# Another written-out order of the cycle of a cross-attention kernel, from sequence 2 on

## The chip, the cores and the metric

The kernel runs on one core of a Trainium2 chip. The metric is the device time of one execution in microseconds (us), the median of several runs.

## What is computed

The layer normalises the input of each of 16 sequences, forms queries from it and keys and values from a context, and adds the attention of 8 heads to the input (cut to what matters; n = 16, c = 64 channels, s = 256 positions, h = 8):

```python
def reference(input, context, gamma, beta, Wq, bq, Wkv, bkv, Wo, bo):
    mu, var = mean(input, axis=(1, 2)), var(input, axis=(1, 2))
    xn = (input - mu) * rsqrt(var + EPS) * gamma[:, None] + beta[:, None]
    q = einsum('oc,ncs->nos', Wq, xn) + bq[:, None]
    kv = einsum('od,nds->nos', Wkv, context) + bkv[:, None]
    ...
    att = softmax(einsum('nhqc,nhkc->nhqk', q * c**-0.25, k * c**-0.25))
    y = einsum('nhqk,nhkc->nhqc', att, v)
    return input + einsum('co,nos->ncs', Wo, y.reshaped) + bo[:, None]
```

## The kernel before, in words

Precision is kept by splitting operands into a high and a low part. For each sequence the work falls into small steps, each a function of the program with the sequence and a head, a unit or a half as arguments. The products of Wq and Wk (t, in `t_a` high and `t_b` low) replace queries and keys, and the products of Wv and Wo (u, in `u_hi` and `u_lo`) replace values and output projection.

TensorE (PE) has `turn_of_t(m, k)` (four matmuls into the bank `ps_t`: t of four heads), `maxima(m, unit)` (one matmul of 512 columns into one of two banks `ps_max`: first scores, from the high parts, only for the row maximum), `transpose_max(m, 0)` (turns the maxima of all heads), `scores(m, head)` (four matmuls into one of two banks `ps_sc`), `values_of_context(m, kt)` (two matmuls into `ps_m`: u), `values(m, first)` (24 short matmuls: the exponentials of two heads by u, into one of two banks `ps_z`) and `transposed_sum(m)` (turns the summed heads into `ps_t`).

ScalarE (ACT) has `t_high` (t_a out of ps_t), `exponentials(m, head)` (two activations over the same scores: `p_hi` in fp16, then `p_full` in fp32), `u_high`, `transpose_out` (the turned maxima, which it then also sends by a DMA of its own queue into a row of `t_b`, so that `scores` subtracts the maximum) and small `inputs`. VectorE (DVE) has `t_low`, `reduce_max(m, unit)`, `u_low`, `reciprocals(m, first)` (of the sums of exponentials of two heads), `add_values(m, first)` (four small instructions that scale and add these two heads) and `residual(m)`. GpSimd (POOL) forms `p_lo` = p_full - p_hi of every head, except for six of the last eleven that DVE does (`p_low`). SyncE (SP) issues all other copies, up to three that replicate t_a within the core (L400, L414), one for t_b (L406), c_pad and c_seq (the context), x_seq and the output. SP waits in program order too, and its order isn't touched.

Sequences overlap. Every engine works through its own written-out list, and semaphores make it wait. For the first two sequences the order comes from tables (`step`); from there on each engine runs `cycle(n)` for n = 1 to 14, then `last(15)`. In a cycle stand steps of the sequences n - 2 to n + 2. `fresh` skips a step that has already been issued. So a cycle is the unit of the steady state, and there are twelve of them between the residual of sequence 0 and that of sequence 12. The waits that matter below:

```python
need(pe, dve_tlo, t_bank_free(turn))      # turn_of_t: t_low of the turn before is done (one bank ps_t)
need(pe, act_p, m * H + head - 1)         # scores: the exponentials two heads before are done
pe.wait_ge(dma_negmax[q], 16 * neg_max_loads(m))   # scores(m, 0): the row of maxima has landed
need(pe, dve_max, m * H + unit - 1)       # maxima: reduce_max two units before is done
pe.wait_ge(dve_max, (m + 1) * H)          # transpose_max: all eight reduce_max of m are done
act.wait_ge(dma_tb[q][k], 16 * fills(m))  # transpose_out, before its DMA: both copies of t_b have landed
dve.wait_ge(dve_inv, m * PAIRS + pair + 1)  # add_values: its own reciprocals are done
```

Of the kernel before, what the change touches and what calls it, by code (L numbers as in the profile page):

```python
# [78 lines left out]
def xattn_program(nc, x2_in, x_tiles_in, ctx2_in, wq_in, wk_in, w_in, out):  # L79
# [4 lines left out]
    with stack:  # L84
# [247 lines left out]
        def fresh(done, kind, index, within=True):  # L332

            if not within or index < done.get(kind, 0) or kind == 't' and index >= PAIRS + 2 * (N - 1):
                return False
            done[kind] = index + 1
            return True
# [89 lines left out]
        def _(pe):  # L427
# [136 lines left out]
            def maxima(m, unit):  # L564

                if not fresh(done, 'max', m * H + unit, 0 <= m < N):
                    return
                q, bank = m % 2, unit % 2
                need(pe, dve_max, m * H + unit - 1)
                if m == 0:  # L570
                    if unit == 0:
                        c_ready(pe, m)
                    if unit < 2:
                        pe.wait_ge(dve_alo, unit + 1)
                    if unit % 2 == 0:
                        pe.wait_ge(act_thi, unit // 2 + 1)
                    for qt in range(KT):
                        last = mm(ps_max[:, bank, qt * S:(qt + 1) * S], t_a[:, q, unit, qt * P:(qt + 1) * P], c_seq[:, m % C_BUFS, 0, :],
                                  start=True, stop=True)
                else:  # L580
                    if unit == 0:
                        pe.wait_ge(dma_cpad[q], 32 * fills(m))
                    if unit % 4 == 0:
                        pe.wait_ge(act_thi, PAIRS + 2 * (m - 1) + unit // 4 + 1)
                    head, qt = unit // 2 * 2, unit % 2
                    last = mm(ps_max[:, bank, :], t_a[:, q, head, qt * P:(qt + 1) * P], c_pad[:, q, :, :].rearrange("p k s -> p (k s)"),  # L586
                              start=True, stop=True)
                last.then_inc(pe_s1, 1)

            def transposed_sum(m):  # L590

                if not fresh(done, 'y', m, 0 <= m < N):
                    return
                pe.wait_ge(dve_zsum, (m + 1) * H * KT)
                need(pe, dve_tlo, min(PAIRS + 2 * (m + 3 - 1) + 2, PAIRS + 2 * (N - 1)))
                nc.tensor.transpose(ps_t[:, 0:P], z_sum[:, m % 2, :, :].rearrange("p t c -> p (t c)"), ident[:]).then_inc(pe_y, 1)  # L596
# [51 lines left out]

            def cycle(n):

                maxima(n + 1, 2)
                maxima(n + 1, 3)
                scores(n, 0)
                values(n - 1, 4)
                scores(n, 1)
                maxima(n + 1, 4)
                maxima(n + 1, 5)
                scores(n, 2)
                values(n - 1, 6)
                transposed_sum(n - 2)  # L660
                scores(n, 3)
                maxima(n + 1, 6)
                maxima(n + 1, 7)
                values_of_context(n + 1, 0)
                turn_of_t(n + 2, 0)
                scores(n, 4)
                values(n, 0)
                maxima(n + 2, 0)
                transpose_max(n + 1, 0)
                maxima(n + 2, 1)  # L670
                scores(n, 5)
                scores(n, 6)
                values_of_context(n + 1, 1)
                values(n, 2)
                scores(n, 7)
                turn_of_t(n + 2, 1)

            def last(n):

                scores(n, 0)  # L680
                values(n - 1, 4)
                scores(n, 1)
                scores(n, 2)
                values(n - 1, 6)
                transposed_sum(n - 2)
                scores(n, 3)
                values_of_context(n, 1)
                scores(n, 4)
                values(n, 0)
                scores(n, 5)  # L690
                scores(n, 6)
                values(n, 2)
                scores(n, 7)
                transposed_sum(n - 1)
                values(n, 4)
                values(n, 6)
                transposed_sum(n)
# [5 lines left out]
        def _(act):  # L703
# [65 lines left out]
            def t_high(m, k):  # L769

                turn = turn_of(m, k)
                if not fresh(done, 't', turn):
                    return
                act.wait_ge(pe_t, turn + 1)
                need(act, pe_s2, (m - 2) * H + 4 * k + 4)
                to = t_a[:, 0, 2 * k:2 * k + 2, :] if m == 0 else packed(t_a, m, k)[:, 0]
                nc.scalar.activation(to, t_bank(turn).rearrange("p (j s) -> p j s", j=2), ACT.Copy).then_inc(act_thi, 1)  # L777
# [48 lines left out]

            def cycle(n):

                t_high(n + 1, 1)
                u_high(n, 1)  # L830
                exponentials(n, 0)
                inputs(n, 0)
                exponentials(n, 1)
                inputs(n, 1)
                exponentials(n, 2)
                inputs(n, 2)
                exponentials(n, 3)
                u_high(n + 1, 0)
                t_high(n + 2, 0)
                inputs(n, 3)  # L840
                exponentials(n, 4)
                transpose_out(n + 1, 0)
                inputs(n, 4)
                exponentials(n, 5)
                inputs(n, 5)
                exponentials(n, 6)
                inputs(n, 6)
                exponentials(n, 7)
                inputs(n, 7)

            run_cycles(step, cycle, cycle)


# [66 lines left out]
        def _(dve):  # L920
# [184 lines left out]

            def cycle(n):

                reduce_max(n + 1, 1)
                add_values(n - 1, 2)
                reduce_max(n + 1, 2)  # L1110
                p_low(n - 1, 7)
                reduce_max(n + 1, 3)
                u_low(n, 1)
                reciprocals(n - 1, 4)
                t_low(n + 1, 1)
                reduce_max(n + 1, 4)
                p_low(n, 1)
                reduce_max(n + 1, 5)
                residual(n - 2)
                add_values(n - 1, 4)  # L1120
                reduce_max(n + 1, 6)
                p_low(n, 3)
                reduce_max(n + 1, 7)
                u_low(n + 1, 0)
                reciprocals(n - 1, 6)
                reciprocals(n, 0)
                add_values(n - 1, 6)
                t_low(n + 2, 0)
                reduce_max(n + 2, 0)
                p_low(n, 5)  # L1130
                add_values(n, 0)
                reciprocals(n, 2)

            def last(n):
# [61 lines left out]
```

## Time and profile before

| | us |
|---|---|
| median of 3 runs | 220.38 (219.92, 220.38, 222.49) |
| the profiled execution | 218.92 |
| its span, first to last instruction | 217.1 |
| twelve cycles, residual to residual | 136.04, so 11.34 each |
| after the twelfth | 22.2 |

The profiled execution is 1.46 below the median of the runs. Its busy shares are PE 93%, DVE 92%, ACT 83%, POOL 75% of the span. A busy PE in this profile is partly a model of the ends of matmuls, so that waits of PE are better read from starts of instructions. The granted TensorE clock is full (1.0) in all of the cycles.

### The profile page before, as it was taken

What the parts mean: (1) busy time and instruction counts of PE and PEld (TensorE: products, weight loads), DVE (VectorE), ACT (ScalarE), POOL (GpSimd) and SP (SyncE); (2) the same over time, 40 slices, a digit from 0 to 9 for tenths busy, and PEclk for the clock granted to TensorE, in tenths of its full rate; (3) what the DMA queues carried; (4) which work ended last, traced back from release to release, by engine and by line L of the source; (5) the groups of instructions that cost most, each with busy time, mean ns of one, the idle gap of its engine ahead of it and who ended that gap; (6) DMA issues with size and microseconds to landing.
All of it is one profiled execution on the core that took longest, in us unless ns stands there. A gap on an engine that the chain in (4) does not pass through costs nothing.

```text
span 217.1 us, 7194 instructions
## 1 busy us (share of the span) xinstructions
PE 202.1 (93%) x2511; PEld 178.1 (82%) x2511; DVE 199.2 (92%) x589; ACT 180.1 (83%) x366; POOL 162.6 (75%) x162
## 2 busy tenths in 40 slices
PE   6987888899999999999999999999999999999882
PEld 6876766788888888898989987988988898988771
DVE  4589998899999999999999999999999999997884
ACT  2365588797989898989899898989898989898980
POOL 5136087896989888888889889889787879786550
PEclk9975899999999999999999999999999999999997
DMA  5963137672765757667566665666666574552000
GB/s 147 295 259 89 37 73 170 140 160 64 161 160 132 168 128 169 139 156 163 133 158 150 160 152 127 147 151 161 145 148 160 127 176 113 128 116 47 2 22 17
DMA packets 31090, 29.04 MB, mean 134 GB/s; under 512 B 4240, under 2 KB 29840, under 8 KB 31056
## 3 DMA queue, kind: packets, MB, share of 16 engines
q1 hardware_dynamic: 30224, 28.07, 54.5%
q10 hardware_dynamic: 832, 0.53, 0.9%
q8 instruction: 20, 0.33, 0.7%
q14 instruction: 14, 0.11, 0.2%
HBM read 3.80 MB, written 1.05 MB: 22 GB/s over the span
## 4 chain that ended last, share of the span: by engine, by line
PE 78%; DVE 8%; ACT 6%; DMA 3%; issue 2%; ACTq 1%; SPq 0%
PE ps_sc L559 16%; PE ps_sc L560 13%; PE ps_max L586 12%; PE ps_z L508 7%; PE ps_z L510 7%; PE ps_z L509 7%; PE ps_m L622 3%; PE ps_m L623 3%; DMA x_res<-x_tiles 3%; PE ps_t L532 3%; PE ps_t L533 3%; ACT p_full L790 2%; DVE neg_max L1020 1%; ACT p_hi L787 1%; PE ps_t L596 1%
## 5 line engine op out<-in xcount | busy, mean ns | idle before, releaser
L913 POOL TENSOR_TENSOR p_lo<-p_full,p_hi 128x512 f16<-128x512 f32 x122 | 139.6, 1166 | 30.4 <-ACT p_full L790 26.3
L787 ACT ACTIVATE p_hi<-ps_sc 128x512 f16<-128x512 f32 x128 | 78.7, 615 | 14.7 <-PE ps_sc L560 13.2
L1020 DVE TENSOR_REDUCE neg_max<-ps_max 128x2 f32<-128x512 f32 x128 | 82.8, 677 | 1.5 <-PE ps_max L586 1.3
L790 ACT ACTIVATE p_full<-ps_sc 128x512 f32<-128x512 f32 x128 | 79.2, 618 | 0.5 <-POOL p_lo L913 0.5
L559 PE MATMUL ps_sc<-t_a,c_seq 128*128 128x256 f32 x256 | 72.4, 306 | 2.4 <-issue 1.6
L560 PE MATMUL ps_sc<-t_b,c_seq 65*128 65x256 f32 x256 | 66.4, 282 | 0.0
L559 PEld LDWEIGHTS ps_sc<-t_a,c_seq 128*128 128x128 f32 x256 | 49.1, 192 | 9.7 <-ACT p_full L790 4.2
L508 PE MATMUL ps_z<-u_hi,p_hi 128*128 128x65 f16 x512 | 53.4, 195 | 1.2 <-DVE p_lo L1066 1.1
L508 PEld LDWEIGHTS ps_z<-u_hi,p_hi 128*128 128x128 f16 x512 | 45.9, 97 | 8.6 <-issue 5.1
L509 PE MATMUL ps_z<-u_lo,p_hi 128*128 128x64 f16 x512 | 52.8, 192 | 0.0
L510 PE MATMUL ps_z<-u_hi,p_lo 128*128 128x65 f16 x512 | 52.7, 193 | 0.0
L560 PEld LDWEIGHTS ps_sc<-t_b,c_seq 65*128 65x128 f32 x256 | 48.8, 190 | 0.9
L1040 DVE SCALAR_TENSOR_TENSOR z_sum<-ps_z,inv_sum,z_sum 128x64 f32<-128x64 f32 x224 | 48.2, 274 | 0.1
L509 PEld LDWEIGHTS ps_z<-u_lo,p_hi 128*128 128x128 f16 x512 | 46.7, 98 | 0.0
L510 PEld LDWEIGHTS ps_z<-u_hi,p_lo 128*128 128x128 f16 x512 | 46.7, 97 | 0.0
L586 PE MATMUL ps_max<-c_pad,t_a 128*128 128x512 f32 x120 | 41.4, 417 | 0.6 <-DVE neg_max L1020 0.2
L1058 DVE TENSOR_TENSOR u_lo<-ps_m,u_hi 128x512 f16<-128x512 f32 x32 | 21.9, 685 | 1.2 <-ACT u_hi L799 1.1
L586 PEld LDWEIGHTS ps_max<-c_pad,t_a 128*128 128x128 f32 x120 | 19.8, 190 | 2.9 <-DVE neg_max L1020 1.5
L1000 DVE TENSOR_TENSOR t_b<-ps_t,t_a 128x512 fp32r<-128x512 f32 (+1 forms) x30 | 20.1, 671 | 0.0
L799 ACT ACTIVATE u_hi<-ps_m 128x512 f16<-128x512 f32 x32 | 19.5, 610 | 0.6 <-PE ps_m L623 0.6
L777 ACT ACTIVATE t_a<-ps_t 128x512 fp32r<-128x512 f32 x30 | 18.3, 608 | 0.0
L532 PE MATMUL ps_t<-x_seq,a_hi 128*128 128x256 f32 x60 | 16.1, 290 | 0.3 <-issue 0.3
(107 smaller groups left out, 231.3 us busy)
## 6 DMA issues: line engine op xcount, KB each, us to landing
t_a<-t_a SPq DMA_DIRECT2D x90, 128.0 KB, 2.5
t_b<-t_b SPq DMA_DIRECT2D x30, 128.0 KB, 2.5
x_seq<-x_hi SPq DMA_DIRECT2D x15, 128.0 KB, 2.4
c_pad<-c_hi SPq DMA_DIRECT2D x30, 64.0 KB, 2.0
c_seq<-c_hi SPq DMA_DIRECT2D x15, 128.0 KB, 2.4
x_res<-x_tiles SPq DMA_DIRECT2D x4, 256.0 KB, 6.2
out<-x_res SPq DMA_DIRECT2D x16, 64.0 KB, 2.1
x_seq<-x_lo SPq DMA_DIRECT2D x15, 64.0 KB, 2.1
```

The costliest lines, as they stand in the source:

```text
L508: mm(ps_z[:, bank, z0:z0 + Z_W], p_hi[:, buf, kt, qs], u_h, start=(kt == 0), stop=False)
L509: mm(ps_z[:, bank, z0:z0 + C], p_hi[:, buf, kt, qs], u_l, start=False, stop=False)
L510: last = mm(ps_z[:, bank, z0:z0 + Z_W], p_lo[:, buf, kt, qs], u_h, start=False, stop=(kt == KT - 1))
L532: mm(bank[:, j * S:(j + 1) * S], a_hi_cols[:, first:first + 2 * C], x_seq[:, q, 0, :], start=True, stop=False)
L559: mm(ps_sc[:, bank, kt * S:(kt + 1) * S], c_seq[:, b, 0, keys], t_a[:, q, head, :], start=True, stop=False)
L560: last = mm(ps_sc[:, bank, kt * S:(kt + 1) * S], c_seq[0:C + 1, b, 1, keys], t_b[0:C + 1, q, head, :], start=False, stop=True)
L586: last = mm(ps_max[:, bank, :], t_a[:, q, head, qt * P:(qt + 1) * P], c_pad[:, q, :, :].rearrange("p k s -> p (k s)"), start=True, stop=True)
L787: nc.scalar.activation(p_hi[:, buf, :, :].rearrange("p t s -> p (t s)"), scores, ACT.Exp).then_inc(act_phi, 1)
L790: nc.scalar.activation(p_full[:, head % 2, :], scores, ACT.Exp).then_inc(act_p, 1)
L913: nc.gpsimd.tensor_tensor(p_lo[:, buf, :, :].rearrange("p t s -> p (t s)"), p_full[:, head % 2, :], p_hi[:, buf, :, :].rearrange("p t s -> ...
L1020: nc.vector.tensor_reduce(to, ps_max[:, unit % 2, :].rearrange("p (t s) -> p t s", t=KT), X, ALU.max, negate=True).then_inc(dve_max, 1)
L1040: nc.vector.scalar_tensor_tensor(out=total, in0=part, scalar=scale, in1=total, op0=ALU.mult, op1=ALU.add).then_inc(dve_zsum, 1)
```

## The change

The three lists `cycle(n)` are written in another order. Nothing is added or removed: the same steps run on the same engines. The list `last(n)` of PE loses `scores(n, 0)`, since the cycle before has it now.

```diff
 PE: def cycle(n):
-                maxima(n + 1, 2)
                 maxima(n + 1, 3)
-                scores(n, 0)
                 values(n - 1, 4)
+                maxima(n + 1, 4)
                 scores(n, 1)
-                maxima(n + 1, 4)
                 maxima(n + 1, 5)
+                transposed_sum(n - 2)
                 scores(n, 2)
+                maxima(n + 1, 6)
                 values(n - 1, 6)
-                transposed_sum(n - 2)
+                values_of_context(n + 1, 0)
                 scores(n, 3)
-                maxima(n + 1, 6)
+                turn_of_t(n + 2, 0)
                 maxima(n + 1, 7)
-                values_of_context(n + 1, 0)
-                turn_of_t(n + 2, 0)
                 scores(n, 4)
                 values(n, 0)
+                transpose_max(n + 1, 0)
                 maxima(n + 2, 0)
-                transpose_max(n + 1, 0)
                 maxima(n + 2, 1)
                 scores(n, 5)
+                values(n, 2)
                 scores(n, 6)
                 values_of_context(n + 1, 1)
-                values(n, 2)
+                maxima(n + 2, 2)
                 scores(n, 7)
                 turn_of_t(n + 2, 1)
+                scores(n + 1, 0)
 ACT: def cycle(n):
-                t_high(n + 1, 1)
-                u_high(n, 1)
-                exponentials(n, 0)
-                inputs(n, 0)
                 exponentials(n, 1)
                 exponentials(n, 2)
+                u_high(n + 1, 0)
                 exponentials(n, 3)
-                u_high(n + 1, 0)
                 t_high(n + 2, 0)
...
                 exponentials(n, 7)
+                t_high(n + 2, 1)
                 inputs(n, 7)
+                exponentials(n + 1, 0)
+                u_high(n + 1, 1)
+                inputs(n + 1, 0)
 DVE: def cycle(n):
-                reduce_max(n + 1, 1)
                 add_values(n - 1, 2)
                 reduce_max(n + 1, 2)
                 reduce_max(n + 1, 3)
-                u_low(n, 1)
+                t_low(n + 1, 1)
                 reciprocals(n - 1, 4)
-                t_low(n + 1, 1)
                 reduce_max(n + 1, 4)
+                residual(n - 2)
+                u_low(n, 1)
                 reduce_max(n + 1, 5)
-                residual(n - 2)
-                add_values(n - 1, 4)
                 reduce_max(n + 1, 6)
+                add_values(n - 1, 4)
+                reciprocals(n - 1, 6)
+                u_low(n + 1, 0)
                 reduce_max(n + 1, 7)
-                u_low(n + 1, 0)
-                reciprocals(n - 1, 6)
+                add_values(n - 1, 6)
                 reciprocals(n, 0)
-                add_values(n - 1, 6)
-                t_low(n + 2, 0)
+                add_values(n, 0)
                 reduce_max(n + 2, 0)
-                add_values(n, 0)
+                reduce_max(n + 2, 1)
+                t_low(n + 2, 0)
                 reciprocals(n, 2)
```

In three places the instructions themselves show it. The line numbers of the changed kernel are one lower from here on for ACT and DVE.

PE at the end of a cycle, before: the turn of t (L532, L533), two maxima (L586), then the scores of head 0 (L559, L560).

```order
L532 MATMUL ps_t<-x_seq,a_hi 128x256
L533 MATMUL ps_t<-x_seq,a_lo 128x256
L532 MATMUL ps_t<-x_seq,a_hi 128x256
L533 MATMUL ps_t<-x_seq,a_lo 128x256
L586 MATMUL ps_max<-c_pad,t_a 128x512 x2
L559 MATMUL ps_sc<-t_a,c_seq 128x256
L560 MATMUL ps_sc<-t_b,c_seq 128x256
```

PE at the same place in the changed kernel:

```order
L532 MATMUL ps_t<-x_seq,a_hi 128x256
L533 MATMUL ps_t<-x_seq,a_lo 128x256
L532 MATMUL ps_t<-x_seq,a_hi 128x256
L533 MATMUL ps_t<-x_seq,a_lo 128x256
L559 MATMUL ps_sc<-t_a,c_seq 128x256
L560 MATMUL ps_sc<-t_b,c_seq 128x256
L559 MATMUL ps_sc<-t_a,c_seq 128x256
L560 MATMUL ps_sc<-t_b,c_seq 128x256
L586 MATMUL ps_max<-c_pad,t_a 128x512
```

Scores of head 0 follow the turn of t at once, one of the maxima comes after them, and the other one has moved ahead of the turn.

ACT where a sequence ends and the next begins, before: the exponentials of head 7, `t_high` (L777), `u_high` (L799), the exponentials of head 0.

```order
L787 ACTIVATE p_hi<-ps_sc 128x512
L790 ACTIVATE p_full<-ps_sc 128x512
L777 ACTIVATE t_a<-ps_t 128x2x256
L799 ACTIVATE u_hi<-ps_m 128x8x64
L787 ACTIVATE p_hi<-ps_sc 128x512
L790 ACTIVATE p_full<-ps_sc 128x512
```

ACT there in the changed kernel:

```order
L786 ACTIVATE p_hi<-ps_sc 128x512
L789 ACTIVATE p_full<-ps_sc 128x512
L776 ACTIVATE t_a<-ps_t 128x2x256
L786 ACTIVATE p_hi<-ps_sc 128x512
L789 ACTIVATE p_full<-ps_sc 128x512
L798 ACTIVATE u_hi<-ps_m 128x8x64
```

`u_high` has moved behind the exponentials of head 0.

DVE in the second half of a cycle, before: from `u_low(n + 1, 0)` (L1058) by the two reciprocals (L1011), `add_values(n - 1, 6)` (L1040), `t_low(n + 2, 0)` (L1000), a reduction (L1020), `add_values(n, 0)` (L1037, L1040), and on to `add_values(n, 2)`.

```order
L1058 TENSOR_TENSOR u_lo<-ps_m,u_hi 128x512
L1011 RECIPROCAL inv_sum<-ps_z 128x4 x2
L1040 SCALAR_TENSOR_TENSOR z_sum<-ps_z,inv_sum,z_sum 128x64 x4
L1000 TENSOR_TENSOR t_b<-ps_t,t_a 128x2x256
L1020 TENSOR_REDUCE neg_max<-ps_max 128x2
L1037 TENSOR_SCALAR z_sum<-ps_z,inv_sum 128x64 x2
L1040 SCALAR_TENSOR_TENSOR z_sum<-ps_z,inv_sum,z_sum 128x64 x2
L1011 RECIPROCAL inv_sum<-ps_z 128x4
L1020 TENSOR_REDUCE neg_max<-ps_max 128x2
L1040 SCALAR_TENSOR_TENSOR z_sum<-ps_z,inv_sum,z_sum 128x64 x4
```

DVE there in the changed kernel:

```order
L1057 TENSOR_TENSOR u_lo<-ps_m,u_hi 128x512
L1019 TENSOR_REDUCE neg_max<-ps_max 128x2
L1039 SCALAR_TENSOR_TENSOR z_sum<-ps_z,inv_sum,z_sum 128x64 x4
L1010 RECIPROCAL inv_sum<-ps_z 128x4
L1036 TENSOR_SCALAR z_sum<-ps_z,inv_sum 128x64 x2
L1039 SCALAR_TENSOR_TENSOR z_sum<-ps_z,inv_sum,z_sum 128x64 x2
L1019 TENSOR_REDUCE neg_max<-ps_max 128x2 x2
L999 TENSOR_TENSOR t_b<-ps_t,t_a 128x2x256
L1010 RECIPROCAL inv_sum<-ps_z 128x4
L1039 SCALAR_TENSOR_TENSOR z_sum<-ps_z,inv_sum,z_sum 128x64 x4
```

Two of the four reciprocals of a cycle now stand directly ahead of the sum that uses them, and `t_low(n + 2, 0)` has moved from before `add_values(n, 0)` to behind it and behind two reductions.

## Rows read from the trace of the kernel before

**Rows 1.** Windows from residual to residual: window, length; busy us of the engines
```profile
58.83:70.23 11.40, 11.37 (x152) 10.11 (x151) 11.13 (x33) 10.48 (x22) 10.29 (x11) 1.00 0.64 150
...
104.39:115.63 11.24, 11.24 (x152) 10.04 (x151) 11.02 (x34) 10.36 (x23) 9.77 (x10) 1.00 0.62 142
...
183.56:194.87 11.31, 11.25 (x152) 10.04 (x151) 11.01 (x33) 10.40 (x22) 9.25 (x9) 1.00 0.56 125
```

**Rows 2.** Timeline of a cycle, ACT and PE: start, us, instruction, idle before
```profile
101.10 0.62 ACT L799 ACTIVATE u_hi<-ps_m 128x512 f16<-128x512 f32 x1
102.05 0.64 ACT L790 ACTIVATE p_full<-ps_sc 128x512 f32<-128x512 f32 x1
102.74 0.19 PEld L559 LDWEIGHTS ps_sc<-t_a,c_seq 128*128 128x128 f32 x1 [0.39 <-ACT p_full L790]
110.11 0.36 PE L559 MATMUL ps_sc<-t_a,c_seq 128*128 128x256 f32 x1
```

**Rows 3.** Timeline of DVE in the same cycle
```profile
101.14 0.68 DVE L1020 TENSOR_REDUCE neg_max<-ps_max 128x2 f32<-128x512 f32 x1
101.75 0.69 DVE L1058 TENSOR_TENSOR u_lo<-ps_m,u_hi 128x512 f16<-128x512 f32 x1
102.35 0.17 DVE L1011 RECIPROCAL inv_sum<-ps_z 128x4 f32<-128x4 f32 x1
102.44 0.66 DVE L1000 TENSOR_TENSOR t_b<-ps_t,t_a 128x512 fp32r<-128x512 f32 x1
...
104.39 0.35 DVE L1049 SCALAR_TENSOR_TENSOR x_res<-ps_t,u_unscale,x_res 128x128 f32<-128x128 f32 x1
104.66 0.85 DVE L1040 SCALAR_TENSOR_TENSOR z_sum<-ps_z,inv_sum,z_sum 128x64 f32<-128x64 f32 x4
105.43 1.28 DVE L1020 TENSOR_REDUCE neg_max<-ps_max 128x2 f32<-128x512 f32 x2
```

**Rows 4.** Timeline of DVE at the end of the kernel
```profile
213.08 0.18 DVE L1011 RECIPROCAL inv_sum<-ps_z 128x4 f32<-128x4 f32 x1
213.30 0.86 DVE L1040 SCALAR_TENSOR_TENSOR z_sum<-ps_z,inv_sum,z_sum 128x64 f32<-128x64 f32 x4
```

**Rows 5.** Timeline of PE, one step of each kind (of values, the first matmul)
```profile
99.93 0.62 PE L586 MATMUL ps_max<-c_pad,t_a 128*128 128x512 f32 x2
100.39 0.28 PE L559 MATMUL ps_sc<-t_a,c_seq 128*128 128x256 f32 x1
...
100.87 0.20 PE L508 MATMUL ps_z<-u_hi,p_hi 128*128 128x65 f16 x1
...
101.60 0.37 PE L559 MATMUL ps_sc<-t_a,c_seq 128*128 128x256 f32 x1
```

**Rows 6.** The copy of the maxima, its scores, and its 15 landings (view of L764)
```profile
130.68 0.54 ACTq L764 DMA_DIRECT2D t_b<-neg_max_rows  x1
...
133.61 0.63 PE L586 MATMUL ps_max<-c_pad,t_a 128*128 128x512 f32 x2
134.69 0.36 PE L559 MATMUL ps_sc<-t_a,c_seq 128*128 128x256 f32 x1 [0.45 <-issue]
...
DMA to landing us min/median/max: 1.8/2.5/3.9
```

**Rows 7.** SP's copies of t_b in two cycles, and their 30 landings (view of L406)
```profile
98.21 0.61 SPq L406 DMA_DIRECT2D t_b<-t_b  x1
...
103.54 0.60 SPq L406 DMA_DIRECT2D t_b<-t_b  x1
...
131.52 0.62 SPq L406 DMA_DIRECT2D t_b<-t_b  x1
...
138.27 0.61 SPq L406 DMA_DIRECT2D t_b<-t_b  x1
...
DMA to landing us min/median/max: 2.4/2.5/4.1
```

**Rows 8.** Timeline of ACT in the last sequence, exponentials of head 3
```profile
205.85 0.60 ACT L787 ACTIVATE p_hi<-ps_sc 128x512 f16<-128x512 f32 x1 [0.23 <-PE ps_sc L560]
```

More of the change, by code:

```diff
@@ L649, in cycle @@
             def cycle(n):
-                maxima(n + 1, 2)
                 maxima(n + 1, 3)
-                scores(n, 0)
                 values(n - 1, 4)
+                maxima(n + 1, 4)
                 scores(n, 1)
-                maxima(n + 1, 4)
                 maxima(n + 1, 5)
+                transposed_sum(n - 2)
                 scores(n, 2)
+                maxima(n + 1, 6)
                 values(n - 1, 6)
-                transposed_sum(n - 2)
+                values_of_context(n + 1, 0)
                 scores(n, 3)
-                maxima(n + 1, 6)
+                turn_of_t(n + 2, 0)
                 maxima(n + 1, 7)
-                values_of_context(n + 1, 0)
-                turn_of_t(n + 2, 0)
                 scores(n, 4)
                 values(n, 0)
+                transpose_max(n + 1, 0)
                 maxima(n + 2, 0)
-                transpose_max(n + 1, 0)
                 maxima(n + 2, 1)
                 scores(n, 5)
+                values(n, 2)
                 scores(n, 6)
                 values_of_context(n + 1, 1)
-                values(n, 2)
+                maxima(n + 2, 2)
                 scores(n, 7)
                 turn_of_t(n + 2, 1)
+                scores(n + 1, 0)
             def last(n):
-                scores(n, 0)
                 values(n - 1, 4)
```

## The prediction

> **What bounds the kernel now.** I read the busy time from residual to residual first. An undisturbed cycle takes 11.24 us, the first of the twelve 11.40, and their mean is 136.04 / 12 = 11.34; in 11.24 us DVE is busy 11.02 and ACT 10.36 [rows 1]. So the reader should see three engines close to full, and ask for the loop that closes a cycle, not for the busiest engine. The timeline shows it: PE stands 0.39 us until `exponentials(n, 0)` is done, starts `scores(n, 2)` about 102.75, and runs from there without a wait to `scores(n, 7)` at 110.11, which is 7.36 us [rows 2]. The other 3.9 us of the loop are ACT's: exponentials of head 7, `t_high`, `u_high`, exponentials of head 0. DVE isn't the bound, only close to it. Its own sum goes by starts: a reduction 0.61, `u_low` 0.60, a reciprocal 0.09, the residual 0.27, the four instructions of `add_values` 0.77 [rows 3]; `t_low` is taken as 0.60 like `u_low`. Eight reductions 4.8 (two in a row take 1.2, so 0.60 each), two `t_low` and two `u_low` 2.4, four `add_values` 3.08, four reciprocals 0.36, residual 0.27: 10.9. DVE waits about 0.34 us a cycle.
>
> **ACT: the old loop opens.** With `u_high(n, 1)` behind the exponentials of head 0, those start 0.47 us earlier (one such start to the next, 0.95 for `u_high` and the first of the two exponentials together) [rows 2]. If nothing else held, a cycle would be 10.8. `u_low(n, 1)` comes later on DVE as well, so nobody waits for `u_high` there.
>
> **DVE: 0.26 us more of its own.** A reciprocal takes 0.09 when something else follows; where its own sum follows it takes 213.30 - 213.08 = 0.22 [rows 3, 4]. Two of four now stand so: +0.26, sum 11.14 a cycle. The waits it has today may go, for `values(n, 0)` and `transposed_sum` now stand further ahead of what needs them. The Trainium skill (VectorE: DVE Perf Modes, "The DRAIN you can't avoid") says that a semaphore after each DVE operation costs nothing extra; by it DVE's sum would stay at 10.9. The rows disagree, and I take the rows.
>
> **A new loop, DVE to PE to DVE.** `turn_of_t(n + 2, 1)` needs the bank that `t_low(n + 2, 0)` reads, and this now comes late on DVE, after `add_values(n, 0)` and two reductions. Behind that turn PE has `scores(n + 1, 0)` and `maxima(n + 2, 3)`, and DVE's `reduce_max(n + 2, 3)` waits for the latter. Call the start of `reduce_max(n + 1, 3)` zero. Until the end of `t_low(n + 2, 0)` DVE does seven reductions 4.2, `t_low` and two `u_low` 1.8, three `add_values` 2.31, three reciprocals 0.40 (one at 0.22), the residual 0.27, and the last `t_low` 0.66: 9.64. Then the turn, four matmuls like scores, 0.48 (from 100.39 to 100.87) [rows 5], up to 0.58 if its first weights are loaded after a wait; scores 0.48; the maximum 0.43 until it can be read (two take 0.62 with starts 0.23 apart, and a little for the signal). With 0.05 to 0.12 for the signal to PE this is 11.08 to 11.25.
>
> **PE nearly fills it too.** By starts [rows 5]: maxima 0.23, scores 0.48, values 0.73, a turn 0.48, the context 0.46, and 0.08 where long weights follow short matmuls. Eight, eight, four, two and two of these, with five of the 0.08 and 0.15 for the two transpositions: 11.0. Laid out from zero, `maxima(n + 1, 3)` starts at -0.43, `scores(n, 3)` at 3.7, `scores(n, 4)` at 4.9, `values(n, 0)` at 5.4; `transpose_max` at 6.1 has to wait for `reduce_max(n + 1, 7)`, which ends at 6.08 and signals by 6.2; the turn is reached at 9.8, when `t_low` has just ended (9.64 and the signal). PE meets DVE within 0.1 us twice a cycle. The closed loop by this path is 11.15 to 11.25. I take 11.22 for the new cycle, in the upper half, since each such meeting can only add. Against 11.24 that is -0.02 x 12 = -0.2 us. The ends are 11.14 (DVE alone: -0.1 x 12 = -1.2) and 11.35 (another 0.1 for the two meetings: +1.3). So the loop of ACT is replaced by another of the same length.
>
> **Queues that are passed: the copy of the maxima.** `scores(n, 0)` waits for the row of maxima that ACT sends. One such copy was issued at 130.68; two maxima started at 133.61, and scores would have followed 0.46 later, at 134.07. They started at 134.69 [rows 6]. The row calls it "issue", but 130.68 + 3.9, the longest landing, is 134.58: it is the landing. The slack is 134.07 - 130.68 = 3.39; three landings of the cycles are longer (3.8, 3.9 and about 3.5), and cost 0.4 + 0.5 + 0.1 = 1.0 us. In the new order: exponentials of head 3 start about 0.7 after their scores (0.48 for four matmuls and the drain of the last), at 4.4; they take 0.96, `t_high` 0.48, those of head 4 0.96, `transpose_out` 0.3. The copy goes out at 7.1, and `scores(n + 1, 0)` is due at 9.64 + 0.12 + 0.53 = 10.3. The slack is 3.2, 0.2 less.
>
> And ACT may not issue it before SP's second copy of t_b has landed. Today SP issues this at 103.54 - 101.14 = 2.4 after zero [rows 3, 7], far ahead. Its chain of copies starts with the other copy of t_b, which must wait for `t_low(n + 2, 0)`, in the new order at 9.64 - 11.22 = -1.6. From the one copy to the other SP takes 5.33 in one cycle and 6.75 in another [rows 7]. So the second goes out at 3.8 to 5.2 and lands (2.5 in the median) at 6.3 to 7.7, against 7.1: up to 0.6 of wait on ACT, 0.2 in the mean. Behind it are queued the exponentials of heads 5 to 7, which have some 0.3 us of slack against PE. With 0.2 less slack and 0.2 more delay, the spread of the landings (three of thirteen at 3.5 to 3.9, one 3.1, nine up to 2.6) gives 0.20 us a cycle in place of 0.08: +1.5. If no landing is long, it is -1.0. What speaks for shorter ones is that SP now stands idle for over a microsecond before `t_low(n + 2, 0)`, so less is under way beside the row. I take the middle, +0.25.
>
> The Trainium skill (DMA: Bandwidth & Descriptors, "Anatomy of one DMA — SWDGE (gpsimd) path") calls the fixed 2 us of a transfer roughly constant, and this row is 8 KB. By it the landing would never matter, and the term would be -1.0. The view has 1.8 to 3.9 for equal copies [rows 6], so the spread, not the fixed part, is what decides here.
>
> **The end.** From `cycle(14)` on no new maxima and turns are left, and ACT is the chain. There `u_high(15, 1)` stood before the exponentials of head 0 as well; PE got `scores(15, 2)` later and ACT still waited 0.23 before head 3 [rows 8]. Moving it gives between 0 and 0.48; I take -0.4, since that wait shows that PE's side was late for it.
>
> **Sum**, against the profiled execution: 218.92 - 0.2 + 0.25 - 0.4 = 218.6. The runs' median is 1.46 above the profiled execution, so 220.0. POOL, the other copies and the first two sequences are set at nothing: the heads' p_lo are due 0.5 us or more after POOL has them, but the margin for `values(n, 2)` shrinks from some 2 us to 0.6, and there its cover ends; one more GpSimd instruction of 0.7 there would cost 0.1.
>
> **Rivals.** (A) DVE alone sets the cycle and no row is late. For it: both meetings are within what the rows resolve, and SP's idle time. -1.2 - 1.0 - 0.4 = -2.6: 216.3, so 217.8 as a median. If the page's rule on semaphores held too, the new loop would lose a further 0.13 a cycle, and 216.2 would be possible. Against it: any 0.1 us of jitter now hits an engine without slack.
>
> (B) Slower: the copy of the maxima becomes the bound. Its place is the wait of `scores(n + 1, 0)`, its cause SP's later copy of t_b, its price 12 times the mean lateness, behind which maxima 3 and DVE's reduction stand. It decides from 0.03 us a cycle above what I took, and is visible (2%) from 0.4. With a lateness of 0.5 in every cycle (landings at 3.4, issue 0.3 late): 12 x 0.5 = 6.0 in place of today's 1.0, so 218.92 - 0.2 + 5.0 - 0.4 = 223.3, as a median 224.8; with half of it 221.8.
>
> (C) The two meetings cost 0.1 us each: +2.4 above the forecast, 222.4. It differs from B by where PE stands: before the turn and before `transpose_max`.
>
> **Chances.** Forecast (a cycle of 11.15 to 11.30, rows late as now) 0.5, A 0.2, B 0.18, C 0.12. The range takes all of A's but its far end, C, and the milder half of B: 217.2 to 223.2. Two per cent is 4.4 us, about what a measurement of this kernel tells from no change. Below 216.0 lies only the far end of A, 0.03; above 224.8 the upper part of B, 0.07; in between 0.9.
>
> **What the changed profile would show.** Residuals 11.22 apart, with no wait of PE before `scores(n, 2)`. DVE busy above 11.1 a cycle: its reciprocals 0.22 apart from their sums twice a cycle. PE reaching `turn_of_t(n + 2, 1)` as `t_low` ends. Copies of the maxima issued 7.1 us after `reduce_max(n + 1, 3)`, scores of head 0 3.2 later; where PE stands longer there, the landing, and ACT idle before this copy, speak for B. I am wrong if DVE's chain or PE's has a wait I put at zero, and most easily if the landings shift as a whole.

## The result, and the profile after

The changed kernel took 222.72 us (median of 4 runs, 221.96 to 224.15), the kernel before 220.15 beside it: a ratio of 1.0111, 95% interval [1.0066, 1.0156]. Two further copies of it, each timed beside before, gave 1.001 [0.997, 1.005] and 1.0091 [1.0047, 1.0134]. The same code thus gives 0.1 to 1.1% in three comparisons, which differ by more than their intervals. It is slower by some tenths of a per cent to one per cent, where 220.0 had been forecast with the sign of a small gain. The profiled execution took 222.15 us, its span 220.3.

I split the spans of this profile, of two others of the same code and of a second one of the kernel before by the residuals, as in [rows 1]:

| profile | span | first residual | twelve cycles | of these the first | a clean cycle | cycles 2 to 12 above clean |
|---|---|---|---|---|---|---|
| before | 217.1 | 58.83 | 136.04 | 11.40 | 11.24 | 1.0 |
| before, repeated (c_before) | 218.4 | 60.23 | 135.89 | 11.47 | 11.24 | 0.8 |
| after | 220.3 | 60.99 | 135.91 | 10.73 | 11.15 | 2.5 |
| after, repeated (c_after) | 219.8 | 57.26 | 139.21 | 10.57 | 11.15 | 6.0 |
| after, repeated (c_after2) | 218.7 | 59.23 | 136.04 | 10.58 | 11.15 | 2.8 |

The last column is the sum of cycles 2 to 12 less eleven clean ones. In the changed cycle the residual stands 1.4 us earlier (1.87 behind `reduce_max(n + 1, 3)`, before 3.25 [rows 3]), that of sequence 0 only 0.8 (3.69 against 4.50). So the starts are better compared by `reduce_max(3, 3)` itself: it begins at 54.3 and 55.8 us in the two profiles of the kernel before, at 57.3, 53.6 and 55.6 in the three of the changed one. Over all fourteen profiles of this document the mean is 55.9 for the old order and 55.9 for the new one: the start varies by itself. From there to the end it is 162.8 and 162.6 us before, and 163.1, 166.2 and 163.1 after. So of the 3.2 us between the first profiles of the two kernels 3.0 lie at the start. What the change did is in the last two columns: **clean cycles got shorter, and the time lost in disturbed ones grew.**

Windows of the changed kernel, columns as in [rows 1]: a clean cycle, and a disturbed one.

```profile
94.54:105.70 11.16, 11.16 (x152) 10.29 (x151) 11.09 (x34) 10.18 (x22) 9.67 (x10) 1.00 0.66 152
...
162.15:173.66 11.51, 11.48 (x152) 10.23 (x151) 11.12 (x35) 10.12 (x22) 9.22 (x9) 1.00 0.64 144
```

DVE is busy 11.09 of 11.16 us, where it was 11.02 of 11.24 [rows 1]: it has its longer sum, and hardly any wait. In the disturbed cycle it is busy for the same time (11.12), and the cycle is 0.35 longer. Why is seen on the timelines of SP, ACT, PE and DVE there:

```profile
163.43 1.90 SPq L414 DMA_DIRECT2D t_a<-t_a  x1
165.38 0.61 SPq L406 DMA_DIRECT2D t_b<-t_b  x1
...
167.03 0.25 ACT L753 ACTIVATE neg_max_rows<-ps_m 16x128 fp32r<-16x128 f32 x1
167.94 0.52 ACTq L763 DMA_DIRECT2D t_b<-neg_max_rows  x1
168.56 0.60 ACT L786 ACTIVATE p_hi<-ps_sc 128x512 f16<-128x512 f32 x1 [1.28 <-PE ps_z L510]
169.06 0.59 ACT L789 ACTIVATE p_full<-ps_sc 128x512 f32<-128x512 f32 x1
...
169.27 0.40 PE L586 MATMUL ps_max<-c_pad,t_a 128*128 128x512 f32 x1
169.70 0.39 PE L559 MATMUL ps_sc<-t_a,c_seq 128*128 128x256 f32 x1
...
171.33 0.40 PE L586 MATMUL ps_max<-c_pad,t_a 128*128 128x512 f32 x1
...
171.77 0.69 DVE L1019 TENSOR_REDUCE neg_max<-ps_max 128x2 f32<-128x512 f32 x1 [0.32 <-PE ps_max L586]
```

SP's second copy of t_b goes out at 165.38, 5.1 behind `reduce_max(n + 1, 3)` (160.28, the residual's 162.15 less 1.87), and needs 2.47: it lands at 167.85. ACT has turned the maxima at 167.03 and could send them 0.28 later, at 167.31, as in the undisturbed cycles. It sends them at 167.94, so 0.63 late and 0.10 behind that landing; in all seven cycles of this profile where ACT sends the row late, it does so 0.10 behind the landing of this copy. So it waited for that. The row of ACT names PE as the releaser of its idle time, but the DMA that stands between is what was waited for. Behind it ACT is 0.63 late: exponentials of head 5 end at 169.65, so `scores(n, 7)` starts at 169.70, where it would follow its maximum after 0.23, at 169.50; then the turn, `scores(n + 1, 0)`, maxima 3, and DVE waits 0.32 for these. Of 0.63 us of ACT's wait, 0.32 reach the cycle.

The other wait is that for the row itself. Where it lands in time, `scores(n + 1, 0)` starts 3.19 us behind the copy's issue (3.40 in the kernel before); here in after and in before:

```profile
99.70 0.52 ACTq L763 DMA_DIRECT2D t_b<-neg_max_rows  x1
...
102.89 0.28 PE L559 MATMUL ps_sc<-t_a,c_seq 128*128 128x256 f32 x1
```

```profile
108.21 0.53 ACTq L764 DMA_DIRECT2D t_b<-neg_max_rows  x1
...
111.61 0.28 PE L559 MATMUL ps_sc<-t_a,c_seq 128*128 128x256 f32 x1
```

And here the row is late, in c_after, ACT and PE:

```profile
85.52 0.52 ACTq L763 DMA_DIRECT2D t_b<-neg_max_rows  x1
...
89.55 0.36 PE L559 MATMUL ps_sc<-t_a,c_seq 128*128 128x256 f32 x1 [0.68 <-issue]
```

The row landed after 3.94 us, at 89.46, and PE started 0.09 later, as it does behind every row that is late. As in [rows 6] it is called "issue". PE waited for such a landing in three of the twelve cycles of before and in four of after, where it cost at most 0.4 each. The summary rows of its two kinds of copy, of L763 (the row) and L406 (t_b), which answer to [rows 6, 7]:

```profile
DMA to landing us min/median/max: 1.8/2.6/3.5
...
DMA to landing us min/median/max: 2.3/2.4/3.6
```

They are like those of before (medians 2.5 and 2.5). ACT's wait before head 3 of the last sequence [rows 8] is gone.

### The profile page after: what moved, and what is told of

It is laid out like the page before. It is cut to its first block, busy times and chain, and to the rows that moved or that the text cites. A ratio compares the mean times of both kernels' runs of the same rounds, so it can differ in the third digit from the quotient of the medians.

```text
span 220.3 us, 7194 instructions
## 1 busy us (share of the span) xinstructions
PE 204.5 (93%) x2511; PEld 183.1 (83%) x2511; DVE 201.2 (91%) x589; ACT 179.1 (81%) x366; POOL 163.4 (74%) x162
## 3 DMA queue, kind: packets, MB, share of 16 engines
q1 hardware_dynamic: 30224, 28.07, 54.3%
## 4 chain that ended last, share of the span: by engine, by line
POOL 52%; issue 18%; PE 13%; DVE 6%; ACT 5%; DMA 3%; ACTq 1%; POOLq 0%; SPq 0%; DVEq 0%
POOL p_lo L912 49%; DMA x_res<-x_tiles 3%; ACT p_full L789 2%; PE ps_sc L559 2%; ACT p_hi L786 1%; PE ps_sc L446 1%; PE ps_sc L560 1%; PE ps_z L508 1%; DVE c_tops L1073 1%; POOL x_lo L882 1%; DVE neg_max L1019 1%; POOL xn L870 1%; ACTq L757 1%; PE ps_max L586 1%; PE ps_z L510 1%
## 5 line engine op out<-in xcount | busy, mean ns | idle before, releaser
L1019 DVE TENSOR_REDUCE neg_max<-ps_max 128x2 f32<-128x512 f32 x128 | 84.0, 680 | 3.8 <-PE ps_max L586 3.4
L559 PE MATMUL ps_sc<-t_a,c_seq 128*128 128x256 f32 x256 | 71.7, 301 | 2.3 <-DMA t_b<-neg_max_rows 0.7
L560 PE MATMUL ps_sc<-t_b,c_seq 65*128 65x256 f32 x256 | 67.4, 284 | 0.0
L559 PEld LDWEIGHTS ps_sc<-t_a,c_seq 128*128 128x128 f32 x256 | 49.0, 191 | 7.7 <-issue 3.8
L560 PEld LDWEIGHTS ps_sc<-t_b,c_seq 65*128 65x128 f32 x256 | 49.0, 191 | 2.8
L586 PE MATMUL ps_max<-c_pad,t_a 128*128 128x512 f32 x120 | 47.4, 419 | 0.2 <-DVE neg_max L1019 0.2
L586 PEld LDWEIGHTS ps_max<-c_pad,t_a 128*128 128x128 f32 x120 | 21.8, 192 | 1.7 <-DVE neg_max L1019 0.9
L532 PE MATMUL ps_t<-x_seq,a_hi 128*128 128x256 f32 x60 | 16.7, 299 | 0.7 <-issue 0.7
```

Source lines behind the costliest of these rows:

```text
L559: mm(ps_sc[:, bank, kt * S:(kt + 1) * S], c_seq[:, b, 0, keys], t_a[:, q, head, :], start=True, stop=False)
L560: last = mm(ps_sc[:, bank, kt * S:(kt + 1) * S], c_seq[0:C + 1, b, 1, keys], t_b[0:C + 1, q, head, :], start=False, stop=True)
L1019: nc.vector.tensor_reduce(to, ps_max[:, unit % 2, :].rearrange("p (t s) -> p t s", t=KT), X, ALU.max, negate=True).then_inc(dve_max, 1)
```

## Experiments

Each ratio is to the kernel before, run in turn with it; "above clean" is the last column of the table.

**Copies of both kernels, and two single moves.** c_before and c_after are unchanged copies.

> The kernel before, unchanged, as a control and for a second profiled execution. The two traces at hand put the whole difference (3.2 us) ahead of the first cycle: u_low of sequence 0 starts at 33.3 and 35.5, the first residual at 58.8 and 61.0, while twelve cycles take 136.0 and 135.9. Theory S (the start is a matter of each execution, by when the granted clock falls): this profile's second u_low starts anywhere from 35 to 38.5, unlike the first profile's, or the times of the runs spread over 3 us. Theory K (the start belongs to the kernel): it starts at 35.4 to 35.6 again, as in the first profile of this kernel. In both, twelve cycles take 135.5 to 136.5.

> The changed kernel, unchanged, as a control. Theory S: second u_low starts anywhere from 35 to 38.5 and the ratio to the kernel before falls toward 1.00 with more runs (0.998 to 1.006). Theory K: it starts at 37.9 to 38.3 again, and the ratio stays at 1.01. Theory C (the cycles cost the time in the executions that were not profiled): twelve cycles take over 137 here. In S and K twelve cycles take 135 to 136.8, with undisturbed cycles of 11.15 and the others lengthened where the scores of head 0 wait for the landing of the maxima.

Measured: c_before 220.56 us, ratio 0.9978 [0.9947, 1.0009]; c_after 221.46, 1.001 [0.997, 1.005]. An unchanged copy differs by 0.2% from its like, and the changed kernel by 1.0% from its first measurement, with intervals that don't meet. So a difference of less than 1% between two comparisons shows little by itself, and I used the profiles for the cause.

**e_max3_first** opens the new loop: maxima ahead of scores, so that DVE's next reduction waits for less.

```diff
 cycle(n), PE, changed kernel
-                maxima(n + 1, 3)
 ...
                 turn_of_t(n + 2, 1)
+                maxima(n + 2, 3)
                 scores(n + 1, 0)
```

> The changed kernel with maxima(n + 2, 3) ahead of scores(n + 1, 0), at the end of PE's cycle. The new loop (t_low, turn of t, scores of head 0, maxima 3, reduce_max 3) loses the 0.48 us of the scores, and a late landing of the maxima no longer holds up DVE's reduction. If that loop and the landing set the changed cycle: undisturbed cycles 11.10 to 11.15 (DVE's own sum), the late ones 0.1 to 0.3 shorter than in the changed kernel, twelve cycles 133.8 to 135.2, so 1 to 2 us faster than the changed kernel. Rival (PE sets the cycle with its own sum): no change, 135.5 to 136.5.

Measured: 222.72 us, 1.0088 [1.0049, 1.0127], so no gain. Its clean cycle is 11.13 as before the edit, DVE busy 11.07 of 11.14: without the loop, DVE's own sum holds it at the same value. Above clean it has 3.9, with 1.3 us of ACT's wait for t_b (see below) and five rows that landed after 3.6 to 4.1. Opening the loop alone didn't bring the 1 to 2 us expected.

**e_uhigh_moved** makes one part of the change alone, on the kernel before: it opens ACT's old loop.

```diff
 cycle(n), kernel before
 ACT
-                u_high(n, 1)
                 exponentials(n, 0)
+                u_high(n, 1)
 DVE
-                u_low(n, 1)
                 reciprocals(n - 1, 4)
                 t_low(n + 1, 1)
                 reduce_max(n + 1, 4)
+                u_low(n, 1)
```

> The kernel before with one part of the change: ACT's u_high(n, 1) behind the exponentials of head 0 (and DVE's u_low(n, 1) behind reduce_max(n + 1, 4)). If ACT's loop set the old cycle of 11.24, this one is 11.0 to 11.1, then held by DVE (10.9 of its own and what is left of its waits), and PE no longer waits 0.39 before the scores of head 2: 2 to 3 us faster than the kernel before. Rival (DVE with its waits was the bound): 11.2 again, no difference beyond 0.5 us.

Measured: 219.80 us, 0.9897 [0.986, 0.9935]. Clean cycles are 11.05 to 11.11. This one part is a gain of 1% (2 to 3 us were expected, the medians differ by 1.1), so the loss lies in the rest.

**ACT's wait for t_b.** I read from each profile, for twelve copies of the row, the time from L753 to the DMA above the 0.28 to 0.30 that it takes otherwise: before 0.2 us in all, after 2.4, c_after 3.3 (the expectations say 2.3 and 3.4), c_after2 1.8, e_uhigh_moved 2.0, e_max3_first 1.3. The next runs move SP's second copy of t_b (`tb_copy` is the wait and the DMA of L406) and leave PE, ACT, DVE and POOL alone. c_after2 is the changed kernel again, beside them.

```diff
 SP, from sequence 3 on (e_after_tb, e_before_tb, e_uhigh_tb)
                 for turn, m, k in turns_at(UP_FIRST, UP_AHEAD, n, h):
+                    if k == 1 and m > 2:
+                        tb_copy(turn, m, k)
                     if m > 0:
                         sp.wait_ge(act_thi, turn + 1)
 ...
                 for turn, m, k in turns_at(TB_FIRST, TB_AHEAD, n, h):
-                    if m > 0:
+                    if m > 0 and not (k == 1 and m > 2):
```

> The changed kernel once more, unchanged, beside the kernel before. If the change costs something of its own, the ratio stands near the 1.011 of its first measurement; if its start happened to be late there, near the 1.001 of the first repetition. I expect 1.002 to 1.006.

> The changed kernel, with SP's second copy of t_b (L406, half k = 1, from sequence 3 on) ahead of the two copies of t_a (L400) and the one of L414: some 1.9 us earlier. Theory T (ACT may not send the row of maxima until this copy has landed; in the two profiles of the changed kernel the time from L753 to L763 is 0.28 us where nothing is late, and up to 0.91 and 1.63, together 2.3 and 3.4 us above that in twelve cycles; the exponentials queued behind have no slack against PE): that time is 0.28 to 0.30 in each cycle, the twelve cycles come to 134.5 to 136, and the kernel is 1 to 2.5 us faster than the unchanged copy beside it (ratio to before 0.992 to 0.998). Theory L (only the row's own landings of up to 4.1 us cost): the wait goes, the time stays within 0.5 us.

> The kernel before with the same move of SP's copy of t_b. There the time from L753 to the row's DMA is 0.28 to 0.34, once 0.50, so theories T and L both give no change: ratio 0.998 to 1.002. If moving the copy had an effect of its own (copies of t_a 0.65 us later), it would show here as a ratio above 1.003.

> The kernel before with u_high(n, 1) behind the exponentials of head 0 (as in e_uhigh_moved, 219.8 us, ratio 0.990), and SP's second copy of t_b early as well. Its profile had 2.0 us of ACT's wait before the row above 0.29 in twelve cycles. Theory T: these go, clean cycles of 11.05 to 11.11 everywhere but where the row lands late, ratio 0.981 to 0.986. Theory L: ratio 0.990 as without it.

| | us | ratio to before | above clean |
|---|---|---|---|
| c_after2 | 222.18 | 1.0091 [1.0047, 1.0134] | 2.8 |
| e_after_tb | 220.49 | 0.9988 [0.9947, 1.003] | 2.2 |
| e_before_tb | 220.54 | 1.0014 [0.9975, 1.0053] | 0.3 |
| e_uhigh_tb | 219.26 | 0.9892 [0.9846, 0.9938] | 2.7 |

Timelines of e_after_tb in the same cycle as above, SP and ACT:

```profile
159.29 0.62 SPq L372 DMA_DIRECT2D t_b<-t_b  x1
159.95 1.27 SPq L408 DMA_DIRECT2D t_a<-t_a  x2
161.33 0.59 SPq L420 DMA_DIRECT2D t_a<-t_a  x1
...
164.01 0.25 ACT L759 ACTIVATE neg_max_rows<-ps_m 16x128 fp32r<-16x128 f32 x1
164.29 0.52 ACTq L769 DMA_DIRECT2D t_b<-neg_max_rows  x1
```

The copy leaves 4.7 us ahead of the turned maxima, where it left 1.65 ahead, and ACT issues the row 0.28 after them, as in all other cycles of this profile (0.28 to 0.29). The changed kernel then takes what before takes: beside c_after2 1% is gained (1.7 us by the medians), while the kernel before, which had 0.2 us of this wait, stays as it was. Theory T expects that, and this is the best evidence for it. Three things limit it. c_after, with the longest of these waits, had a ratio of 1.001 without any edit. The profile of e_after_tb has only 0.6 us less above clean than c_after2's: its 2.2 us are all of the other kind, four rows that landed after 3.3 to 3.8 and kept PE 0.2 to 0.7 us each. And e_uhigh_tb is a miss: ACT's 2.0 us of wait are gone, but the ratio is 0.989 as in e_uhigh_moved, where T expected 0.981 to 0.986. Two rows landed after 4.2 and 4.4 us there, and what its profile has above clean is all of the other kind; whether that hid a gain isn't shown.

**e_before_tb_late** gives the kernel before that wait: the same copy later, behind those of out and of x_hi.

```diff
 SP, from sequence 3 on, kernel before
                     sp.dma_start(x_to[0:C, q, :, :], x_hi_from[half(m), j:j + 1, :].broadcast_to([C, 2, S])).then_inc(dma_xseq[q], 16)
+                    if later:
+                        tb_copy(*later.pop())
 ...
                 for turn, m, k in turns_at(TB_FIRST, TB_AHEAD, n, h):
-                    if m > 0:
+                    if k == 1 and m > 2:
+                        later.append((turn, m, k))
+                    elif m > 0:
 ...
+                if h == 6 and later:
+                    tb_copy(*later.pop())
```

> The kernel before with SP's second copy of t_b (from sequence 3 on) some 2 us LATER, behind the copy of the output and the first of x_seq. Nothing of the compute engines' order changes. Theory T: the time from L753 to the row's DMA, 0.29 us there, grows by 0.3 to 0.6 a cycle in the mean, the row lands later by as much, and the kernel is 1.5 to 5 us slower (ratio 1.007 to 1.023). Theory L (the row's own landing alone): ratio 0.998 to 1.002.

Measured: 237.38 us, 1.0753 [1.0687, 1.0818]. ACT's timeline in one of its cycles:

```profile
149.72 0.27 ACT L767 ACTIVATE neg_max_rows<-ps_m 16x128 fp32r<-16x128 f32 x1
151.89 0.52 ACTq L777 DMA_DIRECT2D t_b<-neg_max_rows  x1
```

ACT waits 1.9 us here (2.17 less the usual 0.28) and 14.7 in twelve cycles; they last 150.6 us in place of 136.0. Direction and place are T's, the size is over three times the upper end. The likely reason, not tested, is that a wait of this length delays the engines that release SP's next copies, and so feeds itself.

**e_recip and e_recip_tlow** ask what closes the clean cycle of 11.15: DVE's sum with its two reciprocals, or the loop through the turn.

```diff
 cycle(n), DVE, e_after_tb
-                add_values(n - 1, 6)
                 reciprocals(n, 0)
+                add_values(n - 1, 6)
                 add_values(n, 0)
                 reduce_max(n + 2, 0)
                 reduce_max(n + 2, 1)
+                reciprocals(n, 2)
                 t_low(n + 2, 0)
-                reciprocals(n, 2)
 e_recip_tlow: t_low(n + 2, 0), reciprocals(n, 2), reduce_max(n + 2, 1)
```

> e_after_tb with reciprocals(n, 0) ahead of add_values(n - 1, 6) and reciprocals(n, 2) ahead of t_low(n + 2, 0), so that no reciprocal stands directly ahead of its own sum. If DVE's own sum (11.14 us) sets the clean cycle of 11.13 to 11.15, this falls by 0.13 for each of two reciprocals to PE's 11.0 to 11.05, and the kernel gains about 1 us against e_after_tb (ratio 0.993 to 0.996). If the new loop DVE - turn - scores - maxima 3 sets it, the loop loses 0.13 and gains 0.09 and the cycle is 11.10 (ratio 0.997).

> e_recip with t_low(n + 2, 0) one step earlier, ahead of reduce_max(n + 2, 1). It opens the new loop by 0.5 us and sends SP's first copy of t_b 0.6 us earlier. If DVE's own sum set the cycle and e_recip reached PE's sum, nothing further: cycle 11.0 to 11.05, ratio as e_recip. If the loop set it, the cycle falls from 11.10 to 11.0 to 11.05, ratio 0.003 to 0.007 below e_recip.

Measured: e_recip 224.39 us, 1.0176 [1.0115, 1.0236], a clean cycle of 11.39; e_recip_tlow 220.27, 0.9973 [0.9936, 1.001], a clean cycle of 11.12 (its profiled execution took 224.56). Both expectations for e_recip fell, and those for e_recip_tlow (11.0 to 11.05) too, though its ratio is 0.02 below e_recip's. DVE in e_recip:

```profile
113.03 0.17 DVE L1016 RECIPROCAL inv_sum<-ps_z 128x4 f32<-128x4 f32 x1
113.12 0.66 DVE L1005 TENSOR_TENSOR t_b<-ps_t,t_a 128x512 fp32r<-128x512 f32 x1
...
115.32 0.69 DVE L1025 TENSOR_REDUCE neg_max<-ps_max 128x2 f32<-128x512 f32 x1 [0.18 <-PE ps_max L592]
...
121.60 0.18 DVE L1016 RECIPROCAL inv_sum<-ps_z 128x4 f32<-128x4 f32 x1 [0.22 <-PE ps_z L516]
```

The reciprocal of head pair 0 now comes before `values(n, 0)` is done and waits 0.22; with the 0.09 of the other one, which now stands ahead of `t_low`, the loop's DVE part grows. From the start of `t_low` (113.12) to the next reduction 3 (115.32) it is 2.20, so of 11.39 the way from reduction 3 to `t_low` takes 9.19, where it takes 8.90 in c_after2. So the loop through the turn is real, and closes the cycle when 0.3 us are added to it. With `t_low` one step earlier it is open, DVE is busy 10.88 of 11.12, its one wait is 0.24 at the same reciprocal, and of PE the view of waits names 0.3 us ahead of two weight loads ("issue"):

```profile
160.76:171.88 11.12, 11.12 (x152) 10.23 (x152) 10.88 (x34) 10.31 (x21) 9.19 (x9) 1.00 0.66 150
```

**e_code_shift** asks why some rows land late. Equal copies of 8 KB land after 1.8 to 4.4 us, the long ones in nearly the same cycles of every profile. Traffic of the instruction queues in two such windows of e_after_tb, from the issue of the row to its landing, some of the queues (packets, MB, share), then the row's landing:

```profile
q8 instruction: 1, 0.02, 2.0%
q10 hardware_dynamic: 32, 0.01, 1.1%
...
t_b<-neg_max_rows ACTq DMA_DIRECT2D x1, 8.0 KB, 3.8
...
q1 hardware_dynamic: 236, 0.20, 45.9%
q10 hardware_dynamic: 32, 0.01, 2.1%
...
t_b<-neg_max_rows ACTq DMA_DIRECT2D x1, 8.0 KB, 1.9
```

The edit is made on e_uhigh_tb; it makes PE's instruction stream 72 instructions longer at the very start (WARM_MEAN is 16).

```diff
-            keep_warm(WARM_MEAN)
+            keep_warm(10)
+            for _ in range(24):
+                mm(ps_z[0:32, 0, 0:8], ident[:, 0:32], mean_w[:, 0:8], start=True, stop=True)
```

> e_uhigh_tb with other idle work of PE at the start: 6 of the 16 warming products fewer, 24 small ones (32 x 8) more, so that PE's instruction stream is some 70 instructions longer ahead of everything else. Of 98 copies of the row in seven profiles, all 27 that landed in 2.7 us or more had a transfer of the instruction queues beside them, and the 45 without one landed in 1.8 to 2.6, in nearly the same cycles from run to run. Theory I (the instruction transfers make the row late): the long landings move to other cycles than 4, 6, 8 and 13, and again each has an instruction transfer beside it; their number may change, and with it the time by up to 2 us either way. Theory N (something of these sequences or buffers makes them late): they stay in the same cycles.

(The 27 there is a miscount; the count below takes its place.) Measured: 221.34 us, 0.9938 [0.9869, 1.0008], too wide to rank it. Its rows of 3.5, 3.6 and 3.1 us are the 3rd, 7th and 12th copy, counted from that of sequence 2; in e_uhigh_tb those of 3.4 and more are the 4th, 8th, 9th and 13th. Each has an instruction transfer beside it, as theory I expects. Over all fourteen profiles 57 of 101 copies with such a transfer within 0.6 us ahead of their issue or before their landing took 2.7 us or more, and none of the 95 others (longest 2.6). A window up to the landing is itself longer for a late row. So I also count by the start of a transfer of queue q8 (16 KB): of 33 rows where one began 0.5 to 1.5 us behind the row's issue, which is ahead of the shortest landing, all 33 took 2.7 us or more; of 55 others where one began in the 2.0 us ahead of the issue, three did.

## Why the prediction was wrong

**Old loop of ACT: right.** Opened alone it gives cycles of 11.05 to 11.11. The estimate of 10.8 had only said what ACT allows; something else, DVE or PE by their sums, stops it at 11.1.

**DVE's sum and the new loop: right.** Reciprocal to sum is 0.21 in the changed profile (167.01 to 167.22), DVE is busy 11.09 a cycle, and the next reduction 3 follows `t_low`'s start by 2.2. Clean cycles are 11.13 to 11.17, inside the 11.08 to 11.25 worked out, and below the 11.22 taken: the 0.07 added for the two meetings of PE and DVE wasn't needed, and rival C is out. Eleven cycles gain 1.0 where 0.2 stood for twelve. The first one seems to gain another 0.7, but most of that is where the residual of sequence 0 stands; from `reduce_max(3, 3)` to `reduce_max(4, 3)` it is 12.63 before and 12.36 to 12.55 after, so 0.1 to 0.3 less, for which I had no term. PE's own sum of 11.0 was probably 0.1 too low for this order: 11.12 stays where DVE has slack and the loop is open (e_recip_tlow). The same steps of PE take 11.05 in the order of e_uhigh_moved, so what holds 11.12 isn't shown.

**Copy of the maxima: this term failed, by its size.** The mechanism had been written down: SP's second copy of t_b goes out at 3.8 to 5.2 and lands up to 7.7, against 7.1; ACT waits 0.2 a cycle in the mean, and exponentials with 0.3 of slack stand behind it. All of that is in the rows: out at 5.1, landed at 7.6; mean wait 0.20, 0.27 and, in c_after2, 0.15; scores of head 0 due 3.19 behind the issue, where 3.2 stood. What was wrong is the price, +0.25 for both parts together, the middle between -1.0 and +1.5. The lower end supposed that SP's idle time would shorten the landings. They run from 1.8 to 4.0, where before has 1.8 to 3.9; the long ones stand beside instruction transfers (e_code_shift), of which the prediction had nothing. In the three profiles (after, c_after2, c_after) the time above clean is 2.5, 2.8 and 6.0 in place of 1.0: +1.5, +1.8 and +5.0, in two of them about the upper end of +1.5 that had been worked out. So rival B, whose place, cause and direction this is, was nearer than the forecast: its times, 221.8 to 224.8, hold two of the three medians, though its price of 0.5 a cycle is reached in c_after alone.

**The end: about right.** From the residual of sequence 12 on, -0.4 was forecast. The residual's own shift is 1.4, and after it the profiles have 23.3 to 23.4 us where before has 22.2, so -0.2 to -0.3.

**Sum.** Cycles -1.0, first cycle -0.2, tail -0.3, time above clean +1.5 to +5.0 (mean 2.8): +1.3 in the mean of three profiles, where -0.4 stood. One by one, from `reduce_max(3, 3)` to the end, they are +0.3, +3.4 and +0.3 above before (after, c_after, c_after2), while the medians of their comparisons say +2.6, +0.5 and +1.4. So the term explains the sign in the mean of the profiles. It does not explain the +2.6 of the first measurement: in its profile 3.0 us are the start, which no term of the change touches, and which stays unexplained. The start goes with TensorE's clock, though not by that alone; windows 10 to 40 us of before, then of after, the granted clock in the third column from the right:

```profile
10.00:20.00 10.00, 8.02 (x54) 7.31 (x54) 8.48 (x26) 7.55 (x15) 6.16 (x10) 0.65 0.56 195
20.00:30.00 10.00, 8.21 (x48) 6.74 (x47) 9.89 (x21) 5.59 (x12) 2.63 (x3) 0.84 0.18 41
30.00:40.00 10.00, 8.40 (x67) 6.51 (x66) 8.69 (x14) 8.06 (x18) 7.45 (x7) 1.00 0.72 164
```

```profile
10.00:20.00 10.00, 7.86 (x52) 7.12 (x51) 8.11 (x25) 7.47 (x15) 6.19 (x10) 0.62 0.65 209
20.00:30.00 10.00, 7.72 (x41) 6.69 (x42) 9.90 (x20) 3.94 (x9) 1.21 (x2) 0.70 0.18 41
30.00:40.00 10.00, 8.02 (x37) 6.22 (x37) 7.57 (x12) 7.70 (x16) 6.83 (x7) 0.83 0.56 129
```

c_after, the same code as after, has 0.64, 0.84 and 1.00 there, like before; c_before, the code of before, has 0.63, 0.68 and 0.83, nearly like after. Straight lines through clock and time of the single runs give 1.0 to 2.6 us less for a mean clock 0.01 higher in the three sets of runs of the kernel before, 1.4 and 0.7 in c_after and c_after2. It is a tendency only: three runs of e_code_shift have a clock of 0.996 or 0.997 and 222.6 us. Whether the late start lowers the clock or the clock makes it late wasn't tried.

The two rules of the Trainium skill came out as the rows had said. "VectorE: DVE Perf Modes" ("The DRAIN you can't avoid") would put a reciprocal ahead of its own sum at no extra cost; 0.21 against 0.09 was measured again. "DMA: Bandwidth & Descriptors" ("Anatomy of one DMA — SWDGE (gpsimd) path") has a fixed 2 us that is roughly constant. It speaks of DMAs that GpSimd issues, these are ScalarE's; most rows agree (1.8 to 2.6), and many of those beside an instruction transfer don't (up to 4.4).

## What to carry to other kernels

When steps move, follow the DMA queue that they feed to the engine that waits for its landing, and price that wait by what is queued behind it; where a term's two ends lie either side of zero, and one of them needs something to get better by itself, don't take the middle. Moving one copy ahead of three others in SP's list took 1% off the changed kernel beside its unchanged copy, and one pair of moved steps (e_uhigh_moved, 219.8 us, 0.9897 [0.986, 0.9935]) is faster than both kernels. An order in which DVE is busy 11.09 of 11.16 us has little room for a late transfer. And where one and the same code differs by 1% between comparisons, repeat it before a small loss is explained.

## What the runs showed of the hardware

- An 8 KB copy from partitions to a row lands after 1.8 to 2.6 us, and up to 4.4 when an instruction queue has a transfer under way: with one, 57 of 101 took 2.7 or more, without one none of 95. What counts is when it starts: all 33 with a 16 KB transfer that began 0.5 to 1.5 us behind their issue were long, three of 55 with one that began ahead. With longer code of PE (e_code_shift, one profile) the long ones were other copies.
- A DMA that an engine issues late for a semaphore shows as idle time of the next instruction, put down to some compute engine (1.28 us "<-PE ps_z" above). The gap ahead of the DMA row is what tells (0.91 in place of 0.28 there).
- A landing of the row that PE waits for is listed as "issue" (0.68 us above).
